# A graph network on one core: two graph convolutions, their picks placed from the ninth group on, the table split beside the first additions, ScalarE's picks and turned rows placed groups later

## What is computed

```python
def gcn_conv(x, edge_index, W, b):
    deg = segment count of col (+ loops); deg_inv_sqrt = rsqrt(deg)
    norm = deg_inv_sqrt[row] * deg_inv_sqrt[col]
    h = x @ W
    out = segment_sum(h[row] * norm[:, None], col)
    return out + b
h = gcn_conv(h0, edge_index, W1, b1)
h = gcn_conv(h, edge_index, W2, b2)
x = x + leaky_relu(h, 0.1)
```

## Time and profile before

| | |
|---|---|
| median of 3 runs | 6289.3 us (6282.28 to 6299.85) |
| the profiled execution | 6298.84 us, span 6296.7 us |
| PE busy | 4473.6 us (71%) |
| DVE busy | 3873.5 us (62%) |
| POOL busy | 4077.7 us (65%) |
| ACT busy | 2370.8 us (38%) |
| mean granted TensorE clock | 0.746 of full |

### The profile page before, as it was taken

The page is one execution under the profiler, slowest core; times in us unless marked ns, Lnnn a source line. Parts: engine busy times, 40 slices in busy tenths (PEclk is TensorE's granted clock), DMA queues, the critical chain, the costliest instruction groups (busy, mean ns, idle before and its releaser), DMA issues. The chain is left out here.

```text
span 6296.7 us, 119222 instructions
## 1 busy us (share of the span) xinstructions
PE 4473.6 (71%) x27040; PEld 3715.4 (59%) x27040; DVE 3873.5 (62%) x13515; ACT 2370.8 (38%) x5196; POOL 4077.7 (65%) x4193
## 2 busy tenths in 40 slices
PE   4556555547777776666687788778888857888886
PEld 2555555437777776666554445544444446887776
DVE  4777777655555555888655555465555545666665
ACT  3555555334444444777300000110000035656662
POOL 2777777427777776444477777377777717777773
PEclk8777777656666666889899889889998975555556
DMA  5555555215555555554222222122222213333332
GB/s 154 158 159 158 159 160 161 64 50 155 155 155 155 156 155 151 167 163 145 53 59 60 61 58 57 44 61 60 61 59 58 55 40 59 59 59 58 59 59 49
DMA packets 753306, 624.32 MB, mean 99 GB/s; under 512 B 350902, under 2 KB 646922, under 8 KB 752650
## 3 DMA queue, kind: packets, MB, share of 16 engines
q0 software_dynamic: 153600, 343.79, 21.2%
q1 hardware_dynamic: 591884, 271.77, 16.2%
q10 hardware_dynamic: 7168, 1.85, 0.1%
HBM read 532.42 MB, written 84.51 MB: 98 GB/s over the span
## 5 line engine op out<-in xcount | busy, mean ns | idle before, releaser
L1213 POOL DMA_INDIRECT sum_rows<-tab_row,src_idx x1472 | 1421.2, 966 | 659.4 <-issue 437.1
L1256 PE MATMUL sum_pX<-sum_mask,sum_part 128*128 128x512 bf16 x4998 | 1170.0, 387 | 60.2 <-DVE sum_mask L1316 60.2
L627 POOL DMA_INDIRECT l_rows<-tab_qv,src_idx x832 | 791.2, 951 | 368.1 <-issue 246.1
L627 POOL DMA_INDIRECT l_rows<-tab_wh,src_idx x832 | 787.3, 946 | 370.8 <-issue 249.3
L1356 DVE TENSOR_TENSOR acc<-acc,sum_pA 128x128 f32 x1664 | 475.1, 285 | 852.9 <-PE sum_pA L1288 792.4
L362 POOL DMA_INDIRECT l_rows<-tab_ax,src_idx x832 | 790.1, 950 | 292.0 <-issue 266.7
L1256 PEld LDWEIGHTS sum_pX<-sum_mask,sum_part 128*128 128x128 bf16 x4998 | 499.8, 100 | 596.2 <-issue 100.1
L677 PE MATMUL l_pA<-l_hotA,l_wrow 128*128 128x128 f32 x3328 | 712.9, 384 | 55.5 <-DVE acc L863 51.9
L649 PE MATMUL l_pK<-l_winr,l_hotT 128*128 128x128 f32 (+1 forms) x3328 | 672.1, 341 | 65.9 <-DVE l_logit L771 44.9
L649 PEld LDWEIGHTS l_pK<-l_winr,l_hotT 128*128 128x128 f32 x3328 | 641.7, 286 | 77.9 <-issue 55.5
L677 PEld LDWEIGHTS l_pA<-l_hotA,l_wrow 128*128 128x128 f32 x3328 | 645.1, 288 | 66.5 <-ACT l_hotA L724 32.9
(11 more groups left out here) (276 smaller groups left out, 7690.4 us busy)
## 6 DMA issues: line engine op xcount, KB each, us to landing
sum_rows_r<-tab_row SPq DMA_DIRECT2D x3584, 0.5 KB
sum_rows_r<-tab_row ACTq DMA_DIRECT2D x3584, 0.5 KB
l_winr<-tab_k SPq DMA_DIRECT2D x832, 64.0 KB
spill<-l_rows SPq DMA_DIRECT2D x104, 512.0 KB
sum_rows<-spill SPq DMA_DIRECT2D x104, 512.0 KB
l_winr<-tab_b SPq DMA_DIRECT2D x840, 32.0 KB
sum_line<-src_lo SPq DMA_DIRECT2D x104, 256.0 KB
sum_rows<-tab_row,src_idx POOLq DMA_INDIRECT x1472
```

Of the source, the lines that this page charges most:

```text
L627: nc.gpsimd.indirect_dma_start(rows[:, g % R, u, :], None, table, bass.IndirectOffsetOnAxis(src_idx[:, t:t + 1], 0)).then_inc(s_rows[g % R ...
L1213: nc.gpsimd.indirect_dma_start(rows[:, g % R, u, :], None, tab_row, bass.IndirectOffsetOnAxis(src_idx[:, t:t + 1], 0)).then_inc(s_rows[g % ...
L1256: last = nc.tensor.matmul(pX[:, k % 2, :], part[:, i, h, :], mask[:, step % MASKS, :], start=h == 0 and i == 0, stop=h == NB - 1 and i == 2)
```

## The change

It does four things, in both convolutions.

1. Picks start at the ninth `f` group (g = 9 is the first with steps) and are spread over 168 groups instead of 178.
2. One of the 7 `r` groups becomes an `f` group (RG = 6, NF = 185): 8 indirect DMAs more, 1024 single-row DMAs fewer in the whole kernel. The `r` groups stand behind `f` group 29 (j + 1).
3. DVE's part of the split moves into the first 7 groups, one portion a group, ahead of the group's additions; the clearing of `acc` and the first groups' additions now stand ahead of it.
4. ACT's `take` is cut in two: the copy out of `pX` one group after the batch is whole, the copy out of `pT` four groups after, each ahead of that group's single rows; PE turns three groups after instead of two, and the x batch is summed behind group `whole + 5`.

```diff
-            XG, RG = 17, 7
+            XG, RG = 17, 6
...
-                return min(XS, -(-(g + 1) * XS // (NF - 6)))
+                return max(0, min(XS, -(-(g + 1 - 9) * XS // (NF - 17))))
...
-                order += [("x", k) for k in range(XG) if whole[k] + 3 == g]
-                order += [("r", j) for j in range(RG) if (j + 1) * 25 == g]
+                order += [("x", k) for k in range(XG) if whole[k] + 5 == g]
+                order += [("r", j) for j in range(RG) if (j + 1) * 29 == g]
...
                             nc.scalar.activation(turned[:], pX[:, k % 2, :], ACT.Copy).then_inc(s_taken, 1)
+
+                        def take_turned(k):
+
                             ae.wait_ge(s_turn, k + 1)
...
                         for g in range(NF):
+                            if g - 1 in whole:
+                                take(whole.index(g - 1))
+                            if g - 4 in whole:
+                                take_turned(whole.index(g - 4))
                             for c in range(done, min(CHUNKS, chunk_at(g + 1))):
                                 rows_one_by_one(ae, G // 2, c)
                             done = min(CHUNKS, chunk_at(g + 1))
-                            if g in whole:
-                                take(whole.index(g))
...
-                                if g - 2 in whole:
-                                    turn(whole.index(g - 2))
+                                if g - 3 in whole:
+                                    turn(whole.index(g - 3))
...
-                        nc.vector.tensor_scalar(p_of[:], minus_p[:], -1.0, None, ALU.mult)
-                        nc.vector.tensor_copy(pI[:, 0:P], iota[:]).then_inc(s_iota, 1)
-                        dve.wait_ge(s_iota, 1)
-                        prepare(0)
-                        prepare(1)
-                        for i in range(GROUPS):
+                        def split(i):
+
                             of = keep[:, i * GB:(i + 1) * GB, :]
...
-                        for g in range(AHEAD):
-                            for step in steps_of(g):
-                                select(step)
+
+                        nc.vector.tensor_scalar(p_of[:], minus_p[:], -1.0, None, ALU.mult)
+                        nc.vector.tensor_copy(pI[:, 0:P], iota[:]).then_inc(s_iota, 1)
+                        dve.wait_ge(s_iota, 1)
+                        prepare(0)
+                        prepare(1)
                         nc.vector.memset(acc[:], 0.0).then_inc(s_add, 1)
...
+                            if kind == "f" and g < GROUPS:
+                                split(g)
                             ahead = list(steps_of(g + AHEAD)) if kind == "f" and g + AHEAD < NF else []
                             dve.wait_ge(s_sum, q + 1)
```

## The result

The changed kernel has a median of 6217.34 us over 4 runs (6211.79 to 6220.4), the kernel before 6288.62 us (6282.28 to 6299.85): a ratio of 0.9879, 95% interval 0.986 to 0.9897, or 71 us less. The forecast was 6225, within 6201 to 6260.

The account below looks back on a forecast made before the run. POOL's indirect DMAs (1.264 us each) were taken as the bound, with waits and tail added. Per convolution -18 -24 +5 +5 = -32, both -64: 6289.3 - 64 = 6225 us, range 6201 to 6260.

Parts of the forecast that it names:

- What bounds the kernel: Both convolutions: POOL is never early, 1.264 us per indirect DMA, 5.06 a group; waits, slow start and tail come on top.
- POOL's waits, -18: POOL's real waits on PE, 37 us in all, would go: 18 us less a convolution.
- the third rival: Change does not reach POOL; its waits and tail stay, ACT late for another reason: 6280 to 6309 us, chance 0.06.
- The tail, 29.2 to 5: From POOL's end to the last addition in each convolution: 29.2 us falls to 5, 24 less.
- The split, +5 between 0 and +9: DVE's 14 spread-out split instructions lengthen POOL's early DMAs: 5 us more a convolution, between 0 and 9.
- One f group more, +5: Four more indirect DMAs on POOL in each convolution, at 1.264 us: 5 us more.
- The sum: All terms of a convolution added: 32 us less each, 64 us less for both.
- PE carries the rest: With denser picks PE needs 4.27 us a group, under POOL's 5.06; the ring of 8 groups covers its waits.
- the first rival: PE's small half-clock lags add up, so POOL waits again, 20 to 28 us a convolution: 6247 to 6280 us, chance 0.12.
- the second rival: PE's clock stays low from the ninth group on; below 0.84 PE is the bound; at 0.75, 6390 us; chance 0.06.
- Waits for single rows: PE's waits for the six r groups' rows: some 35 us a convolution, the first 10 us because SP loads later.
- ACT has no slack: ACT needs 55.2 us a batch against POOL's 53, so its lateness reaches POOL beyond the ring's 40 us.

Follow-up runs that it names:

- b_rg6_act: Changed kernel with the start put back (picks from group 0 over 179 groups, split ahead of everything): 6223.9 us, ratio 0.9895.
- b_r26: Kernel before with r groups behind f group 26 (j + 1) instead of 25 (j + 1): 8368.67 us on the slow chip, 6197.11 us on another.
- b_rg6: Kernel before with RG = 6, r groups behind f group 30 (j + 1): 8187.16 us on the slow chip, 6221.98 us on another.

## Why the prediction was right, point by point

- **What bounds the kernel.** Right: POOL's pace is the floor. Shown by XG = 18, 20 and 21, each of which shortens POOL's run by about what its missing DMAs take.
- **POOL's waits, -18.** Measured 18.4 to 0.0. With that the third rival, that the change does not reach POOL, is out.
- **The tail, 29.2 to 5.** Measured 5.4. It holds 1.6 us of landing, a sum at half clock (granted 0.50) that takes 2.05 instead of the 1.1 I had put in, and DVE's 1.55.
- **The split, +5 between 0 and +9.** Measured +3.0 (9.3 against 6.3), and 2 to 3 by b_rg6_act. The Trainium skill ("SBUF — State Buffer", "SBUF: two separate sides") states that a VectorE instruction with two SBUF inputs and a GpSimd instruction that reads SBUF exclude each other for the whole length of the one that started first. If each of the 14 instructions held POOL for all of its 1.09 us, the cost would be an estimated 15.3 us; the trace agrees in kind, not in size: 13 DMAs are longer, by 9.3 us together, and none by more than 0.87. Why the hold is shorter than the instruction no run shows.
- **One f group more, +5.** POOL's run went from 953.4 to 941.9, -11.5; -18.4 + 3.0 leaves +3.9 for four DMAs.
- **The sum.** Forecast -32 a convolution, measured -35.3 and -34.5, and 71 us for the kernel against 64.
- **PE carries the rest.** Right, with a mean granted clock of 0.96 from 3110 us to the end, where 0.84 was needed; the lags of the first rival did not reach POOL. In the first groups the grant is 0.50, the lower of its two levels, with PE busy for 11.5 of 37 us, as the second rival had it. It rises with the picks, and behind the last of them it is 0.50 again, with PE busy for 14.8 of 30 us:

```profile
3960.00:3990.00 30.00, 14.84 (x60) 13.14 (x60) 11.79 (x35) 0.60 (x1) 21.70 (x23) 0.50 0.20 52
```

  Between the two PE waits for POOL's rows again and again, with the end 100 times from 3110 us on, 0.85 us in the mean, and keeps the full clock; behind each of its four long waits for single rows (5.1 to 13.3 us) the sum took 2.04 or 2.05 us, half clock, instead of some 1.06. The Trainium skill tells in "TensorE: Matmul & The Clock Gate", "HAM oscillation", of a kernel whose matmuls fall back to half clock at every wait on a DMA. The trace agrees for the four long waits and not for the short ones, which are shorter than the waits of the kernel that the Trainium skill tells of.
- **Waits for single rows: forecast 35 us in six, measured 29.9 in four.** The first, forecast at 10 us and put on SP, took 13.3. The traces tell it apart: SP's 256th single row (16 + 160 + 80) is issued at 3183.12 + 38.62 = 3221.7, ACT's about 9 us earlier, and the sum starts at 3222.8.

```profile
3183.12 38.62 SPq L1177 DMA_DIRECT2D sum_rows_r<-tab_row  x80
```

  From POOL's first DMA that is 175 us, where I had 3235 - 3063 = 172 for the rows to be there. None of the waits reached POOL.
- **Where the gain came from.** The forecast gave the start +5 and no gain, and everything to ACT. Right in the whole; but I called ACT's load the cause ("ACT has no slack"). b_r26 shows that this step was only half right: with the load unchanged and the demand one to seven groups later, waits and tail went as far down. The last chunk of each r group was issued in the very step behind which PE asked for it. A later due date cures that, and so does a smaller load together with the divided `take`: in the change the dates are as tight as before (steps 29 to 176, asked behind 29 to 174), and the waits are a third. The 55.2 us that I held against POOL's 53 belong to a batch with 112 single rows; others have 96. In the mean it is 1792 / 17 = 105 rows, 49 us, and with 3 for the copies 52. The rest of ACT's lateness was its standing in `take` for PE. And of the seven waits for single rows the first two were as much SP's: both engines ended within about 1 us of each other there. So that the forecast came out well from ACT's load alone is in part luck: the change moved both load and `take`, and either account gives POOL's waits and the tail to it.
- **The price of the start alone** I had at 0 to 20 us a convolution (after the run on the slower chip); it is 39. The prediction's own +5 for the split holds only where ACT's lateness has been cured.

## What to carry to other kernels

When an engine that is busy for three quarters of a stretch is still never early, add the gaps between its instructions to it: POOL's 0.94 us DMAs with 0.30 us between them made a bound that its busy share of 72% before and 76% after did not show. Then a wait elsewhere is worth something only if it, with those shortly before it, uses up the ring in front of that engine, or if it stands at the end. No single wait was as long as the ring's 40 us, yet several in a row made POOL stand twice: of 167 us of PE's waits in a convolution, 42 counted. And before taking work from a helper that is late, look at when its work is asked for: moving the due date by one group in 25 gave as much as the whole change, without touching what anybody does.

## What the runs showed of the hardware that I had not expected

One chip took 8456.4 us for the kernel before where three others took 6279 to 6289. In b_rg6's profile there ACT issues 96 single rows in 74.93 us, 0.78 each, where the same kernel on the other chip needs 44.01 us for 96, 0.46 each. Over the whole first convolution it is 0.74 against 0.46 us a row for ACT, and 0.87 against 0.48 for SP. POOL's indirect DMAs have the same median of 944 ns.

```profile
4064.50 74.93 ACTq L1177 DMA_DIRECT2D sum_rows_r<-tab_row  x96
```

```profile
3341.96 44.01 ACTq L1177 DMA_DIRECT2D sum_rows_r<-tab_row  x96
```

So single rows are dearer there by 60% for ACT and by 80% for SP, and POOL, which waits for nothing in this kernel on the other chip, waits 285 us for PE. The engine that comes last is SP: at the last r group SP ends issuing at 4987.23 + 117.41 = 5104.6, ACT at 5021.02 + 53.95 = 5075.0, and PE's sum starts at 5105.8.

```profile
4987.23 117.41 SPq L1177 DMA_DIRECT2D sum_rows_r<-tab_row  x160
```

```profile
5021.02 53.95 ACTq L1177 DMA_DIRECT2D sum_rows_r<-tab_row  x80
```

```profile
5105.78 2.05 PE L1288 MATMUL sum_pA<-sum_hot,sum_rows_r 128*128 128x128 f32 x8 [27.23 <-DMA sum_rows_r<-tab_row]
```

Taking away 256 of the 1792 rows that each of the two issues in a convolution gives 269 us instead of 57. The order of the edits changes with it: on that chip RG = 6 gives 3.3%, the later due date 1.0%, and the start alone nothing either way, while on the usual ones the first two are about level and the start costs 1.5%. The chip is slower outside the convolutions too: the first one starts at 3704.7 us instead of 3055.9. Why it is slower no run shows.
